# Turning attention results by VectorE block transposes instead of TensorE, with folded value biases and another order of events

## The chip, the cores and the metric

The kernel runs on one core of one Trainium2 chip. The metric is the device time of one execution in microseconds (us); the median of three runs is compared. A core has TensorE (PE, whose weight loads are listed as PEld), VectorE (DVE), ScalarE (ACT), GpSimd (POOL) and SyncE (SP), each with its own in-order queue of instructions, and semaphores between them.

## The reference

A decoder layer on `x` (4 batches x 512 tokens x 256) with a context of 4 x 1024 x 256: causal self attention, cross attention (16 heads of 16 each), and a mixture of 8 experts with the top 2 taken per token, each followed by a layer norm over the sum with its input.

```python
def _attn(q_in, k_in, v_in, wq, bq, wk, bk, wv, bv, wo, bo, causal):
    Q = (q_in @ wq + bq).reshape(Bq, Sq, H, HD)
    Kp = (k_in @ wk + bk).reshape(Bq, Sk, H, HD)
    V = (v_in @ wv + bv).reshape(Bq, Sk, H, HD)
    scores = jnp.einsum('bqhd,bkhd->bhqk', Q, Kp) / jnp.sqrt(jnp.float32(HD))
    ...
    a = jax.nn.softmax(scores, axis=-1)
    o = jnp.einsum('bhqk,bkhd->bqhd', a, V).reshape(Bq, Sq, Dm)
    return o @ wo + bo
x = _layernorm(x + _attn(x, x, x, ..., True), ln1_g, ln1_b)
x = _layernorm(x + _attn(x, ctx, ctx, ..., False), ln2_g, ln2_b)
x = _layernorm(x + _moe(x, ...), ln3_g, ln3_b)
```

All numbers are float32. Since the weights `a` of a row sum to 1, the value bias `bv` reaches the result as the constant row `bv @ wo`.

## The kernel before

**Work and tiles.** Attention is done in 32 units: 4 batches x self/cross x 4 groups of 4 heads (`UNIT_LIST`). A unit has key tiles of 128 keys: 4 in self attention, 8 in cross attention. For each unit

- `max` events: PE multiplies queries by keys into one of two PSUM slots (`v_slot`, L868/L872), DVE takes row maxima out of it (L1101), POOL and a transpose put them into the operand stack (`max_parts`, `max_rows`, `rows_in`).
- `score` events: PE computes one head's (or several heads') transposed scores of a key tile into one of three banks (`a_bank`, L896), ACT takes the exponential into `probs` (L1041).
- `weigh` events: PE adds the key tile's weighted values into `o_bank` (L913), four heads in four groups of 32 partitions (16 values, one sum of weights, 15 unused), 512 queries in the free dimension. There is one `o_bank`: the first `weigh` of the next unit waits until the last result was copied out.
- `o_out`, right behind a unit's last `weigh`: ACT copies `o_bank` to `o_sb` (L1051).
- `o_turn`, later: PE turns `o_sb` by four 128x128 transposes into a `v_slot` (L921), so that queries are in the partitions; DVE takes the reciprocal of the sums (L1120) and multiplies into `y` (L1123).

After a batch's fourth unit of a kind comes `att_turn`: PE turns `y` back by eight 128x128 transposes into two `a_bank`s (helper `transpose_y`, L816), ACT copies them to `o_t` and adds the value bias (L992). Then `out` multiplies `o_t` by `wo` (L935), DVE adds the residue (L1134), `stats` and `norm` do the layer norm, and `norm_turn` turns its result by the same helper for the next projection (`split`, L836, or `route`, L968). A `split` also goes through ACT (L1010, L1011), POOL (L705 to L709) and six DMAs into the operand stacks.

**Order.** All five queues walk through one list, `ORDER`. It is written out by hand as the string `STEPS`, one letter an event, each letter taking the next event of its track: `m` a maximum, `e` a score, `w` a weigh, `o` an `o_turn`, `r` `rows_in`, `a`, `k`, `v` projections, `s` and `c` the chains behind self and cross attention (which begin with `att_turn`). Other events are put behind named ones, `o_out` behind a unit's last `weigh` among them; `late_loads` issues the DMAs of `wo`, the result biases and others on SP behind the first three `rows_in`. The counters that tell which slot an event uses are worked out from this list in `Numbers`.

At the end, attention of the last batch runs into the experts: `weights` (steps of the routing weights, between DVE and ACT, L523 to L548) stands behind the last score, the last two `o_turn` behind the last `weigh`, then `att_turn`, then `first_row` (DVE copies a row tile, L1410, PE turns it, L1375), then `out`.

## Time and profile before

| | us |
|---|---|
| three runs | 999.18, 1001.68, 1002.14 (median 1001.68) |
| span of the profiled execution | 1004.4 |
| PE busy | 964.6 (96%), 6070 matmuls |
| DVE busy | 560.9 (56%), 957 instructions |
| ACT busy | 584.4 (58%), 1208 instructions |
| POOL busy | 340.8 (34%), 466 instructions |

The span runs from the first to the last instruction of one execution; no other time of that execution is shown, so its span is what sums are made against. "Busy" is the union of an engine's instructions. A matmul of float32 data shows as two instructions, a transpose as one. Matmuls overlap, since the next starts while the last one drains, so the mean duration of one is longer than the distance between two starts; the distance is what a matmul costs in a queue that is full. Attention ends with the start of the last `out` at 695.76 us; the rest is layer norm, routing and experts.

### The profile page before, as it was taken

The page shows a single profiled execution, that of the slowest core. Times are in us where ns is not written, and L with a number is a line of the kernel's source. Part 1 is how long each engine was busy: PE and PEld are TensorE (multiplying, and loading weights), DVE is VectorE, ACT ScalarE, POOL GpSimd, SP SyncE. Part 2 cuts the span into 40 slices and gives each one's busy share as a digit, 9 for nine tenths or more (in the row PEclk, how much of TensorE's full clock was granted, in tenths as well). Part 3 has the DMA queues.
Part 4 walks back from the last instruction along what each step waited for, and adds up shares of the span by engine and source line. Part 5 has one row for each costly group of instructions (what it writes and reads, how often), then busy time and mean ns, then how long its engine had stood idle before and what let it go on. Part 6 is the DMA issues. An engine that isn't in the chain of part 4 may idle for free.

```text
span 1004.4 us, 18852 instructions
## 1 busy us (share of the span) xinstructions
PE 964.6 (96%) x6070; PEld 577.6 (58%) x6071; DVE 560.9 (56%) x957; ACT 584.4 (58%) x1208; POOL 340.8 (34%) x466
## 2 busy tenths in 40 slices
PE   7899889999999999999999999999999999999995
PEld 4455534533445554434544354324888999999974
DVE  4637577787667677777777777852431222111216
ACT  3365456677766567776667866786333444444442
POOL 4465954233504542316254036021341111111115
PEclk9999999999999999999999999999999999999998
DMA  7633443002303201302515022011031443324116
GB/s 218 154 86 92 115 123 95 22 3 81 99 2 86 74 22 44 95 2 80 184 51 166 6 64 75 2 49 48 27 80 49 147 136 125 104 76 159 48 53 214
DMA packets 72013, 84.33 MB, mean 84 GB/s; under 512 B 10758, under 2 KB 65542, under 8 KB 71814
## 3 DMA queue, kind: packets, MB, share of 16 engines
q1 hardware_dynamic: 63820, 64.19, 22.3%
q0 software_dynamic: 5504, 17.34, 5.1%
q10 hardware_dynamic: 2624, 1.97, 0.7%
q8 instruction: 37, 0.61, 0.3%
q14 instruction: 28, 0.23, 0.1%
HBM read 38.89 MB, written 12.63 MB: 51 GB/s over the span
## 4 chain that ended last, share of the span: by engine, by line
PE 87%; DMA 4%; POOL 3%; DVE 2%; ACT 1%; issue 1%; SPq 1%; DVEq 0%; ACTq 0%; POOLq 0%; another core or an unknown queue 0%
PE o_bank L913 15%; PE a_bank L896 15%; PE v_slot L1393 12%; PE v_slot L868 11%; PE a_bank L1385 10%; PE a_bank L836 6%; PE v_slot L872 3%; PE o_bank L1385 3%; PE a_bank L851 3%; PE v_slot L935 3%; PE a_bank L816 1%; PE v_slot L873 1%; DMA stack_or_weights<-parts 1%; PE v_slot L921 1%; DVE max_q L1101 1%
## 5 line engine op out<-in xcount | busy, mean ns | idle before, releaser
L1101 DVE TENSOR_REDUCE max_q<-v_slot 128x1 f32<-128x1024 f32 (+3 forms) x352 | 399.1, 1172 | 100.4 <-PE v_slot L868 64.0
L1041 ACT ACTIVATE probs<-a_bank 128x512 f32<-128x512 f32 (+1 forms) x688 | 361.8, 589 | 114.0 <-PE a_bank L896 109.2
L1399 ACT ACTIVATE hidden<-a_bank,b 128x128 f32<-128x128 f32 x216 | 79.0, 367 | 147.8 <-PE a_bank L1385 127.1
L896 PE MATMUL a_bank<-q_stack_cross,k_stack_cross 99*128 99x512 bf16 x512 | 164.2, 381 | 0.5 <-ACT probs L1041 0.2
L868 PE MATMUL v_slot<-k_stack_cross,q_stack_cross 96*128 96x512 bf16 x512 | 148.6, 379 | 2.0 <-DMA q_stack_cross<-parts 2.0
L1393 PE MATMUL v_slot<-stack_or_weights,hidden 128*128 128x256 f32 x576 | 130.4, 379 | 1.1 <-DVEq L1225 1.1
L913 PE MATMUL o_bank<-probs,v_cross 128*32 128x512 f32 x1024 | 130.3, 602 | 0.0
L1393 PEld LDWEIGHTS v_slot<-stack_or_weights,hidden 128*128 128x128 f32 x576 | 106.6, 190 | 14.3 <-DVEq L1225 1.3
L1385 PE MATMUL a_bank<-x_col,stack_or_weights 128*128 128x128 f32 x864 | 109.2, 276 | 4.5 <-issue 2.4
L1385 PEld LDWEIGHTS a_bank<-x_col,stack_or_weights 128*128 128x128 f32 x864 | 104.8, 192 | 7.5 <-issue 5.6
L896 PEld LDWEIGHTS a_bank<-q_stack_cross,k_stack_cross 99*128 99x128 bf16 x512 | 44.5, 97 | 112.0 <-ACT probs L1041 66.5
L1546 POOL DMA_INDIRECT token_out<-y_row,to_i x28 | 26.7, 955 | 178.5 <-DVE y_row L1428 178.5
L868 PEld LDWEIGHTS v_slot<-k_stack_cross,q_stack_cross 96*128 96x128 bf16 x512 | 47.7, 98 | 62.6 <-issue 12.4
L705 POOL TENSOR_TENSOR rest<-rest,parts 128x512 f32<-128x512 f32 x39 | 45.1, 1156 | 95.0 <-ACT parts L1011 94.9
L1404 DVE COPY x_col<-v_slot 128x256 f32<-128x256 f32 x37 | 15.7, 425 | 106.5 <-PE v_slot L1375 99.8
L726 POOL CAST max_p<-max_q 128x16 bf16<-128x16 f32 x32 | 6.6, 208 | 185.8 <-DVE max_q L1101 185.8
L872 PE MATMUL v_slot<-stack_or_weights 96*128 96x128 bf16 (+3 forms) x256 | 59.9, 304 | 6.5 <-DMA stack_or_weights<-parts 2.8
L715 POOL TENSOR_SCALAR_AFFINE_SELECT probs<-probs 128x512 f32<-128x512 f32 x64 | 39.9, 637 | 58.0 <-ACT probs L1041 55.9
L896 PE MATMUL a_bank<-stack_or_weights 99*128 99x512 bf16 (+3 forms) x256 | 54.3, 302 | 2.9 <-DMA stack_or_weights<-max_t 2.5
L913 PEld LDWEIGHTS o_bank<-probs,v_cross 128*32 128x32 f32 x1024 | 23.1, 108 | 56.1 <-issue 28.7
L873 PE MATMUL v_slot<-mask_q,ident_b 128*128 128x128 bf16 x256 | 49.4, 222 | 0.0
L709 POOL TENSOR_TENSOR parts<-rest,parts 128x512 bf16<-128x512 f32 x39 | 45.4, 1164 | 3.1
(212 smaller groups left out, 1106.0 us busy)
## 6 DMA issues: line engine op xcount, KB each, us to landing
k_stack_cross<-parts SPq DMA_DIRECT2D x96, 128.0 KB, 2.4
stack_or_weights<-in_e_w SPq DMA_DIRECT2D x12, 1024.0 KB, 6.5
stack_or_weights<-parts SPq DMA_DIRECT2D x91, 128.0 KB, 2.4
q_stack_cross<-parts SPq DMA_DIRECT2D x48, 128.0 KB, 2.6
inputs<-in_ctxT POOLq DMA_DIRECT2D x4, 1024.0 KB, 6.6
stack_or_weights<-in_e_w SPq DMA_DIRECT2D x8, 512.0 KB, 4.2
x_slots<-slots_in SPq DMA_DIRECT2D x30, 129.0 KB
y_got<-token_out SPq DMA_DIRECT2D x11, 256.0 KB, 8.0
```

What stands on the lines that cost most here:

```text
L709: nc.gpsimd.tensor_tensor(parts[i][:, 2, :], rest[i][:, :], parts[i][:, 1, :], ALU.subtract).then_inc(split_done, 1)
L836: last = nc.tensor.matmul(bank[:, :], w[wname][:, kk, ch * P:(ch + 1) * P], src[:, kk, t0:t0 + S], start=(kk == 0), stop=(kk == DC - 1))
L868: last = nc.tensor.matmul(slot[:, half * S:(half + 1) * S], lhs, k_stack[1][0:KR, G * u + j, half * S:(half + 1) * S], start=True, stop=True)
L872: nc.tensor.matmul(slot[:, at:at + keys], lhs, k_stack[0][0:KR, G * u + j, 0:keys], start=True, stop=False)
L873: last = nc.tensor.matmul(slot[:, at + keys - P:at + keys], ident_b[:, :], mask_q[:, :], start=False, stop=True)
L896: last = nc.tensor.matmul(bank[:, i * cols:(i + 1) * cols], lhs, q_stack[kind][0:KM, G * u + j, q0:S], start=True, stop=True)
L913: last = nc.tensor.matmul(o_bank[32 * j:32 * (j + 1), q0:S], v_ext[kind][:, kt, at:at + 2 * HD], probs[NO.tile[n, kt] % PB][:, j, q0:S], s ...
L1041: nc.scalar.activation(probs[tile % PB][:, js[0]:js[-1] + 1, q0:S], a_bank[at % AS][:, 0:len(js) * (S - q0)].rearrange("p (j t) -> p j t", ...
L1101: nc.vector.tensor_reduce(most, rows, X, ALU.max, negate=True).then_inc(v_free, 1)
L1385: last = nc.tensor.matmul(h_bank[f % HB][:, 0:P], w1[i][:, c, f * P:(f + 1) * P], x_col[:, c, :], start=(c == 0), stop=(c == DC - 1))
L1393: last = nc.tensor.matmul(y_bank[:, 0:D], hidden[:, f, :], w2[i][:, f, :], start=(f == 0), stop=(f == FC - 1))
L1399: nc.scalar.activation(hidden[:, f, :], h_bank[f % HB][:, 0:P], ACT.Gelu, bias=b1[:, bass.ds(e * FC + f, 1)]).then_inc(flow.gelu_done, 1)
```

## The change

1. `o_out` goes from ACT to DVE: one block transpose of the whole `o_bank` (128 partitions x 512, each 32x32 block turned in place) into `o_tr`, an SBUF tile.
2. `o_turn` has no PE part and no `v_slot` any more. DVE takes the reciprocal of 16 sums and multiplies 256 numbers as before, but from `o_tr`, and writes in blocks of 32 queries to `o_n`, a view of `y`.
3. `att_turn` has no PE and no ACT part: DVE turns `o_n` back by two block transposes of 128x512 into `o_t`. `out` waits for these (`turned`).
4. The value biases are no longer added. A new event `value_biases` behind the fourth `rows_in` has ACT spread the two biases over 128 columns (4 instructions), PE multiply them by the two `wo` (4 matmuls of 256 columns), and DVE add the result to the rows of result biases `out_b`. `add_bias` of batch 0 on POOL waits for it.
5. The rows of `wo` and the value biases are permuted on the host so that two groups of heads share a block (`heads_in_blocks`).
6. `STEPS` is another string of the same events.

```diff
-            if k in ("max", "max_rows", "o_turn", "out", "route", "place"):
+            if k in ("max", "max_rows", "out", "route", "place", "value_biases"):
                 self.v[ev] = v
                 v += 1
...
@@ attention_gpsimd, add_bias
                     if b == 0:
                         pool.wait_ge(const_in, 16 * N_LOADS)
+                        pool.wait_ge(v_free, NO.v["value_biases",] + 1)
@@ attention_tensor
+                elif k == "value_biases":
+                    slot = v_next(ev)
+                    pe.wait_ge(rows_made, 2 * DC)
+                    pe.wait_ge(const_in, 16 * N_LOADS)
+                    for i, wname in enumerate(("sa_wo", "ca_wo")):
+                        for kk in range(DC):
+                            last = nc.tensor.matmul(slot[:, i * D:(i + 1) * D], bias_rows[:, i, kk, :], w[wname][:, kk, :], start=(kk == 0), stop=(kk == DC - 1))
+                    last.then_inc(v_full, 1)
...
-                elif k == "o_turn":
-                    n = ev[1]
-                    slot = v_next(ev)
-                    pe.wait_ge(o_out, n + 1)
-                    for q in range(QT):
-                        last = nc.tensor.transpose(slot[:, q * P:(q + 1) * P], o_sb[n % 2][:, q * P:(q + 1) * P], ident[:, :])
-                    last.then_inc(v_full, 1)
-                elif k == "att_turn":
-                    b, kind = ev[1:]
-                    pe.wait_ge(v_free, NO.v["o_turn", UNIT_NO[b, kind, UNITS - 1]] + 1)
-                    transpose_y(kind, NO.a[ev])
                 elif k == "out":
                     b, kind = ev[1:]
-                    pe.wait_ge(a_free, NO.a["att_turn", b, kind] + DC)
+                    pe.wait_ge(turned, DC * NO.turned[b, kind])
@@ attention_scalar
-                elif k == "o_out":
...
-                    sc.wait_ge(pv_done, NO.last_pv(b, kind, u) + 1)
-                    nc.scalar.activation(o_sb[n % 2][:, :], o_bank[:, :], ACT.Identity).then_inc(o_out, 1)
-                elif k == "att_turn":
-                    other_biases()
-                    to_o_t(NO.a[ev], "ca_bv" if ev[2] else "sa_bv")
+                elif k == "value_biases":
+                    other_biases()
+                    for i, n in enumerate(("sa_bv", "ca_bv")):
+                        for ch in range(DC):
+                            nc.scalar.activation(bias_rows[:, i, ch, :], ident[:, :], ACT.Identity, scale=0.0, bias=bias[n][:, ch:ch + 1]).then_inc(rows_made, 1)
@@ attention_vector
+                elif k == "o_out":
+                    n = ev[1]
+                    b, kind, u = UNIT_LIST[n]
+
+                    if n >= 2:
+                        dve.wait_ge(o_done, NO.o[n - 2] + 1)
+                    dve.wait_ge(pv_done, NO.last_pv(b, kind, u) + 1)
+                    nc.vector.transpose(o_tr[n % 2][:, :], o_bank[:, :]).then_inc(o_out, 1)
                 elif k == "o_turn":
...
+                    if kind and b == 0 and u == 0:
+                        dve.wait_ge(v_full, NO.v["value_biases",] + 1)
+                    dve.wait_ge(o_out, n + 1)
+                    heads = o_tr[n % 2][:, :].rearrange("p (n e) -> p n e", e=BLOCK)
+                    nc.vector.reciprocal(recip[n % 2][:, :], heads[:, :, HD]).then_inc(recip_done, 1)
+                    recips += 1
+                    dve.wait_ge(recip_done, recips)
+                    half = u % 2
+                    nc.vector.tensor_tensor(o_n[kind][:, u // 2, :].rearrange("p (n e) -> p n e", e=BLOCK)[:, :, half * HD:(half + 1) * HD],
+                                            heads[:, :, 0:HD], recip[n % 2][:, :].unsqueeze(2).to_broadcast([P, S // BLOCK, HD]),
+                                            ALU.mult).then_inc(o_done, 1)
+                elif k == "att_turn":
+                    b, kind = ev[1:]
+
+                    reader = NO.read_before[b, kind]
+                    if reader and reader[0] == "split":
+                        dve.wait_ge(a_full, NO.a[reader] + 1)
+                    elif reader:
+                        dve.wait_ge(v_full, NO.v[reader] + 1)
+                    dve.wait_ge(o_done, NO.o[UNIT_NO[b, kind, UNITS - 1]] + 1)
+                    for ch in range(DC):
+                        nc.vector.transpose(o_t[:, ch, :], o_n[kind][:, ch, :]).then_inc(turned, 1)
+                elif k == "value_biases":
+                    dve.wait_ge(v_full, NO.v[ev] + 1)
+                    slot = v_slot[NO.v[ev] % VS][:, 0:2 * D].rearrange("p (k d) -> p k d", k=2)
+                    nc.vector.tensor_tensor(out_b[:, :, :], slot, out_b[:, :, :], ALU.add).then_inc(v_free, 1)
@@ kernel
+def heads_in_blocks(v):
+
+    return v.reshape(DC, 2, G, HD, -1).swapaxes(1, 2).reshape(v.shape)
```

The first line of `STEPS`, before and after (13 lines in all; each letter stands as often as before, in another order):

```diff
-    "aavvaammmmmmammmrkmmmmaeeeammermeemewmeemeemweewweeemmmreemeeeemewwwwmmeaemoeeraeveeweeoeekwwweeemmeeemeememeemwowwwmmmra"
+    "aavvaammmmmmaammmrkmeememeemeeeewmmmeemwmreemweawemeeeeweeemrwwwaememaoemmeemeemeewemwomrmemeeemmeeemeweeweeewommrmwwwosa"
```

## Rows read from the trace of the kernel before

**Rows 1.** The page: busy time and share of PE; the chain by engine.

```profile
PE 964.6 (96%) x6070; PEld 577.6 (58%) x6071; DVE 560.9 (56%) x957; ACT 584.4 (58%) x1208; POOL 340.8 (34%) x466
...
PE 87%; DMA 4%; POOL 3%; DVE 2%; ACT 1%; issue 1%; SPq 1%; DVEq 0%; ACTq 0%; POOLq 0%; another core or an unknown queue 0%
```

**Rows 2.** Busy time by stretch: attention, the rest (engine busy, instructions, granted clock).

```profile
0.00:695.76 695.76, 674.24 (x4148) 310.93 (x4150) 479.12 (x663) 457.32 (x861) 278.99 (x403) 1.00 0.27 77
695.76:1004.40 308.64, 290.35 (x1922) 266.70 (x1922) 81.75 (x294) 127.05 (x348) 61.85 (x63) 0.99 0.31 100
```

**Rows 3.** Groups by shape (busy us, mean ns | idle before): what is removed.

```profile
L921 PE MATMUL v_slot<-ident,o_sb 128*128 128x128 f32 x128 | 19.7, 276 | 0.5 <-ACT o_sb L1051 0.5
L1051 ACT ACTIVATE o_sb<-o_bank 128x512 f32<-128x512 f32 x32 | 19.1, 598 | 20.1 <-PE o_bank L913 19.6 <-issue 0.3
L935 PE MATMUL v_slot<-self_weights,o_t 128*128 128x256 f32 x64 | 14.6, 380 | 0.0
L816 PE MATMUL a_bank<-ident,y_cross 128*128 128x128 f32 x64 | 8.4, 273 | 0.9 <-DVE y_cross L1123 0.9
L992 ACT ACTIVATE o_t<-a_bank,b_sa_bv 128x512 f32<-128x512 f32 x8 | 5.1, 684 | 0.9 <-PE a_bank L816 0.8
```

**Rows 4.** Timeline of PE around one `o_turn` (start, us, what).

```profile
305.84 0.60 PE L921 MATMUL v_slot<-ident,o_sb 128*128 128x128 f32 x4
306.28 0.33 PE L896 MATMUL a_bank<-stack_or_weights 99*128 99x384 bf16 x1
```

**Rows 5.** Groups by shape: DVE instructions nearest to the added ones.

```profile
L1101 DVE TENSOR_REDUCE max_q<-v_slot 128x1 f32<-128x1024 f32 x256 | 302.4, 1220 | 65.9 <-PE v_slot L868 64.0 <-issue 0.9
L1404 DVE COPY x_col<-v_slot 128x256 f32<-128x256 f32 x37 | 15.7, 425 | 106.5 <-PE v_slot L1375 99.8 <-remote 4.6 <-issue 2.1
L1101 DVE TENSOR_REDUCE max_q<-v_slot 128x4 f32<-128x512 f32 x16 | 11.1, 694 | 19.9 <-PE v_slot L873 19.8
L1120 DVE RECIPROCAL recip<-v_slot 128x16 f32<-128x16 f32 x32 | 8.2, 258 | 27.6 <-PE v_slot L921 21.4 <-PE a_bank L896 5.2
L1123 DVE TENSOR_TENSOR y_cross<-v_slot,recip 128x256 f32<-128x256 f32 x16 | 6.8, 424 | 0.6
```

**Rows 6.** Who waited for whom over the span (us in total, times, longest).

```profile
PEld a_bank L896 <- ACT probs L1041: 76.1, 126, 0.8
DVE max_q L1101 <- PE v_slot L868: 64.0, 107, 3.1
PEld v_slot L868 <- DVE max_q L1101: 9.2, 16, 0.8
```

**Rows 7.** Waits of others for the copy out of `o_bank`, L1051.

```profile
  PEld o_bank L913: 0.5, 1
```

**Rows 8.** Busy time, the 20 us stretch with a busy DVE (third number of busy).

```profile
640.00:660.00 20.00, 20.00 (x115) 5.98 (x113) 16.93 (x15) 15.87 (x30) 0.00 (x0) 1.00 0.01 2
```

**Rows 9.** Timeline of all engines at the end of attention.

```profile
689.50 1.64 PE L913 MATMUL o_bank<-probs,v_cross 128*32 128x512 f32 x12
690.34 0.26 DVE L534 TENSOR_REDUCE top_val<-logits 128x12 f32<-128x96 f32 x1 [14.34 <-ACT top_val L529]
691.07 0.66 PE L921 MATMUL v_slot<-ident,o_sb 128*128 128x128 f32 x4
...
692.07 0.18 DVE L548 TENSOR_TENSOR top_val<-top_val 128x12 f32<-128x12 f32 x1
...
692.98 0.26 DVE L1120 RECIPROCAL recip<-v_slot 128x16 f32<-128x16 f32 x1
693.27 0.42 DVE L1123 TENSOR_TENSOR y_cross<-v_slot,recip 128x256 f32<-128x256 f32 x1
693.61 0.28 DVE L1410 COPY x_row<-inputs 128x256 f32<-128x256 f32 x1
...
694.68 0.38 PE L1375 MATMUL v_slot<-ident,x_row 128*128 128x128 f32 x2
...
695.76 3.72 PE L935 MATMUL v_slot<-w_ca_wo,o_t 128*128 128x256 f32 x16 [0.70 <-ACT o_t L992]
```

**Rows 10.** Timeline of SP's queue: last of the late loads, fourth `rows_in`.

```profile
53.09 0.47 SPq L601 DMA_DIRECT2D router_b<-in_router_b  x1
...
66.09 0.76 SPq L612 DMA_DIRECT2D stack_or_weights<-max_t  x1
```

More of the change, by code:

```diff
@@ L38 @@
 SPLITS = 10
+BLOCK = 32
 AHEAD_ROWS = 4
@@ L192, in in_order @@
     order = spread
-    for step, behind in ((("result_biases",), ("norm_turn", B - 1, 0)), (("weights",), ("score", len(UNIT_LIST) - 1, ET - 1, score_groups(1, ET - 1)[-1], True)), (("pads",), ("choose", B - 2)), (("first_row",), ("att_turn", B - 1, 1)), (("experts", 0), ("norm", B - 1, 1)), (("experts", 1), ("route", B - 1)),
+    for step, behind in ((("value_biases",), ("rows_in", len(LATE))), (("result_biases",), ("norm_turn", B - 1, 0)), (("weights",), ("score", len(UNIT_LIST) - 1, ET - 1, score_groups(1, ET - 1)[-1], True)), (("pads",), ("choose", B - 2)), (("first_row",), ("att_turn", B - 1, 1)), (("experts", 0), ("norm", B - 1, 1)), (("experts", 1), ("route", B - 1)),
                          (("rank",), ("experts", 1)), (("experts", 2), ("rank",))):
@@ L218, in __init__ @@
                 a += 1
-            elif k in ("att_turn", "norm_turn"):
+            elif k == "norm_turn":
                 self.a[ev] = a
                 a += DC
+            elif k == "o_turn":
+                self.o[ev[1]] = len(self.o)
+            elif k == "att_turn":
+                self.turned[ev[1:]] = len(self.turned) + 1
+                self.read_before[ev[1:]] = reader
+            if k in ("out", "route") or k == "split" and ev[2] >= 8:
+                reader = ev
             if k == "split":
```

58 lines of the change are left out of this document (27 added, 31 removed).

## The prediction

> **What bounds the kernel now.** I read the page's busy times and its chain first, then busy time by stretch, then groups by shape, then who waited for whom, last the timelines of single places. The reader is to see PE at 96% of the span and on 87% of the chain that ended last, every other engine below 60% [rows 1]. By stretch it is plainer: while attention runs (0 to 695.76 us) PE is busy 674.2 us, DVE 479.1 (69%), ACT 457.3 (66%), and the clock granted to PE is full, 1.00 [rows 2]. So what leaves PE's queue shortens the time, as long as no other queue steps into its place. Behind 695.76 the change touches nothing but the start of the last `out`.
>
> PE's busy time hides short waits: its weight loads waited 76.1 us in total for the exponentials on ACT, in 126 places of at most 0.8 us, mostly while the last matmul drained [rows 6]. DVE on the contrary waited for PE's maxima 64.0 us in 107 places, and PE for DVE's slots 9.2 us in 16 (cross units; self units not counted here) [rows 6]. DVE has room, on the average.
>
> **Removed from PE.** The `o_turn`s are 32 x 4 = 128 transposes. Their busy time is 19.7 us [rows 3], but in a full queue four of them take 306.28 - 305.84 = 0.44 us from start to next start [rows 4]: 32 x 0.44 = 14.1 us. The `att_turn`s are 8 x 8 = 64 of the same shape (half of two groups like the L816 row of [rows 3]; the other half is `norm_turn` and stays): 64 x 0.11 = 7.0 us. Together 21.1 us; by busy time it would be 19.7 + 8.4 = 28.1, which is the upper end.
>
> **Added to PE.** `value_biases` is 4 matmuls of 256 columns, shown as 8; 64 such take 14.6 us [rows 3], so 8 x 0.23 = 1.8 us. Its waits: the late loads, whose last is issued at 53.09, 13 us before the fourth `rows_in` at 66.09, behind which the event stands [rows 10]; in the new list some 12 us of PE work lie between the third and the fourth. I take no wait; were the landing 5 us late, 5 us. Queued behind that wait on PE is everything, so nothing hides it. POOL's first `add_bias` then waits for it too, with splits and masks behind; in the new list `out` of batch 0, which needs the sum, is 14 us of PE work later. The four ACT instructions write 128 columns each; below 4 x 0.6 (the 512-column one of [rows 3]), and `y_cross`, where they write, is otherwise first written in cross attention. Nothing. DVE's sum is one instruction more, 0.7. PE's net is 21.1 - 1.8 = 19.3 us.
>
> **Moved from ACT to DVE.** ACT loses 32 copies of 0.598 and 16 of 0.684 [rows 3], 19.1 + 10.9 = 30 us of its 457. DVE gains 32 block transposes out of PSUM and 16 out of SBUF, each 128x512; the `o_turn` pair (0.258 + 0.424 [rows 5]) stays. The trace has no such transpose. From below: a DVE copy of 256 columns takes 0.425, the reduction of 512 columns 0.694 [rows 5]; a fast copy of 256 columns 0.28 [rows 9], so not below 0.56. From above: as dear as a reduction of 1024 columns, 1.22 [rows 5]. I take 0.69, since one pass over 512 columns is what it is. 48 x 0.69 + 0.7 = 34 us: DVE 479 + 34 = 513 in some 678 us, 76%. In its busiest stretch (16.93 of 20 us [rows 8]) it comes to about 90%.
>
> The Trainium skill speaks to this price and to the change itself: "VectorE: DVE Perf Modes", The three transpose paths, gives 311 ns for a VectorE transpose of 128x128 bf16, in 32x32 blocks only, against 390 on TensorE, and its rules for kernel authors send a 128x128 transpose to TensorE. Four such would be an estimated 1.24 us, near my upper end; no row here has the operation. The 390 is a latency: this trace has 0.276 as the mean and 0.11 as what a transpose costs in a full PE queue [rows 3, 4]. By the page's figures the sum is that of the second rival below.
>
> **The wait that is added.** PE's first `weigh` of the next unit now waits for DVE, where the transpose stands behind maxima, instead of ACT. Before, PE waited 0.5 us once for that copy [rows 7]. I counted PE work in the new list between a unit's last `weigh` and the next unit's first: 31 gaps, from 0.64 to 24 us, median 1.9 (before 3.0); 16 are below 2.0, 18 below 3.2. With DVE idle 0.8 is needed; two gaps of 0.64 then cost 0.3 together. With one maximum under way, 1.22 + 0.69 + 0.1 = 2.0 is needed, and the gaps fall short by 7.2 us in all. But in the new list a last `weigh` (1.0 us) nearly always has another `weigh` or two scores ahead of it and no maximum within the last 1.4 us, so the DVE is mostly free when it ends. I take a quarter: 2 us. While DVE stands waiting for `pv_done`, maxima wait behind it, but PE has one slot more free than before, since `o_turn` uses none. DVE's `att_turn` waits for the last reader of `o_t`, an event earlier on PE; nothing.
>
> **The end of attention.** Here nothing covers the chain, and the reader has to walk it [rows 9]. Before: last `weigh` done at 691.07, `out` starts at 695.76. After, DVE does the steps of `weights` first (they stand before the last `weigh`; the last ends at 692.07 + 0.18 = 692.25), and only then the transpose (692.94), two pairs of reciprocal and product (from 692.98 to 693.27 to the end at about 693.71, so 0.73 each: 694.40), two transposes (695.78), the row copy 0.28 (696.06), and PE's two transposes of that row with the semaphores, 0.4: `out` at 696.45. That is 0.7 later than before, though PE lost 0.44 x 2 + 0.87 = 1.75 there that stands in my 21.1. Correction: -2.45. With transposes at 1.22 it is another 1.6.
>
> **Sum.** 19.3 - 2.45 - 2 = 14.9 us off the profiled span: 1004.4 - 14.9 = 989.5. The runs' median lies 2.7 below that span (1001.68), so I forecast 986.8, say 986. Bounds of it: net PE 26 instead of 19 by busy time, 980; a wait for loads or dearer transposes, 992.
>
> The order itself I cost at nothing: PE works through the same multiplications, and DVE's and ACT's shares by stretches of 25 us look alike but for DVE's gain. That is the weakest term.
>
> **Rivals.**
>
> 1. *ACT's relief comes through too, 977.* ACT has 30 us less, and PE's loads waited 76 us for it [rows 6]. If an eighth of those waits, 9.5 us, was real and goes, the time is 986.5 - 9.5. For: at 640 to 660 ACT and DVE are both near 80% or more [rows 8]. Against: the waits are short and lie under draining matmuls, and DVE grows as ACT shrinks.
> 2. *The block transpose costs 1.22.* 48 x 0.53 = 25 us more on DVE, 79% busy, near 100% in its full stretches. If a third comes through, 8.5, and 1.6 at the end: 986.5 + 10 = 997. For: nothing in the trace shows a transpose. Against: one pass over the data.
> 3. *DVE holds `o_bank`: slower, 1012.* If at each last `weigh` two maxima are queued on DVE, 2 x 1.22 + 0.69 + 0.1 = 3.2 us are needed, 18 gaps are short of it, by 27.5 us in all. 1004.4 - 16.9 + 27.5 - 2.7 = 1012. It decides from 16.9 / 31 = 0.55 us of stall per unit. For: the median gap shrank from 3.0 to 1.9. Against: the maxima stand earlier in the list, and PE's wait for ACT in the same place was 0.5 in all [rows 7].
> 4. *The new order loses what the rest gains, about 1001*: a row of maxima or a load that lands late in the first 70 us, where PE was not full.
>
> **How the numbers follow.** Forecast (981 to 992) 0.60; rival 1 0.14; rival 2 0.12; rival 3 0.10, of which half is above 1005; rival 4 0.04. The likeliest gives 986. A measurement of this kernel can tell about 0.3%, 3 us, from no change: below 998.7 is faster. Forecast and rival 1, and most of 2, lie there: 0.85; same 0.06 (rival 4, the mild end of 2 and 3); slower 0.09. The range that leaves out no more than 2 in 10 goes from 975 (rival 1) to 999 (rival 2 and the mild end of 3).
>
> **What would show it.** Right: PE's busy time in attention down by about 19 us or more, no L921, 64 transposes at L816 instead of 128; DVE transposes near 0.7 us; the last `out` starting about 15 us sooner, and the stretch behind it the same 308.6 us [rows 2]; waits of PE for the transpose out of `o_bank` of 1 to 4 us in sum. Wrong: transposes above 1 us; many waits of the first `weigh` for DVE; PE idle where `value_biases` stands; a change of over 2 us behind the last `out`.

## The result: 0.9% slower, where 1.6% faster was forecast

The changed kernel took 1009.92 us (median of 5 runs, 1008.03 to 1015.29) beside 1001.69 (5 runs of the kernel before on the same chip, 999.18 to 1003.67): ratio 1.0088, interval 1.0063 to 1.0113. The forecast was 986 (975 to 999). The profiled execution has a span of 1007.9 us against 1004.4.

The page of the kernel after: busy time by engine, and the chain that ended last.

```profile
PE 959.8 (95%) x5886; PEld 556.0 (55%) x5887; DVE 594.2 (59%) x1006; ACT 561.2 (56%) x1164; POOL 341.9 (34%) x466
...
PE 85%; DVE 4%; DMA 4%; POOL 2%; issue 2%; ACT 1%; SPq 1%; DVEq 0%; POOLq 0%; ACTq 0%
```

Its busy time by stretch, cut where the last `out` (L948 now) starts. The columns are as in [rows 2].

```profile
0.00:699.18 699.18, 667.34 (x3965) 286.83 (x3966) 511.51 (x710) 434.96 (x818) 280.01 (x403) 0.99 0.27 76
699.18:1007.90 308.72, 292.50 (x1923) 269.15 (x1922) 82.72 (x296) 126.26 (x346) 61.94 (x63) 0.98 0.32 101
```

Set beside [rows 1, 2]: attention ends 3.4 us later, and the stretch behind the last `out` is as long as before (308.7 against 308.6), though the two are not made alike: after the change 3.0 us of it are lost to half clock, before it none. PE has 183 instructions less there, and yet its busy time fell by 6.9 us, not by 19, since a matmul's busy time stretches with the clock and with the ones before it. DVE rose by 32.4 us, as forecast (34). ACT fell by 22.4, less than my 30.

The groups of the kernel after that answer to [rows 3, 5]: `o_turn`'s PE transposes are gone, and these came.

```profile
L1122 DVE STREAM_TRANSPOSE o_tr<-o_bank 128x512 f32<-128x512 f32 x32 | 22.8, 712 | 13.9 <-PE o_bank L937 13.5
L1138 DVE TENSOR_TENSOR y_cross<-o_tr,recip 128x256 f32<-128x256 f32 x16 | 9.5, 595 | 0.5
L1138 DVE TENSOR_TENSOR y_self<-o_tr,recip 128x256 f32<-128x256 f32 x16 | 8.1, 509 | 0.6
L1151 DVE STREAM_TRANSPOSE o_t<-y_cross 128x512 f32<-128x512 f32 x8 | 5.2, 688 | 0.3 <-DVE route_space L511 0.2
```

The price of a block transpose was foreseen: 0.712 us out of PSUM and 0.688 out of SBUF, against 0.69, so the second rival's 1.22 didn't come about. The product, costed at the 0.424 of [rows 5], has a mean of 0.55.

Who waited for whom over the span of the kernel after (total us, times, longest), answering to [rows 6, 7].

```profile
PEld a_bank L920 <- ACT probs L1053: 99.0, 173, 0.8
DVE max_q L1107 <- PE v_slot L884: 52.5, 94, 3.3
PEld v_slot L884 <- DVE max_q L1107: 12.4, 25, 0.8
```

PE's loads now wait 99.0 us for the exponentials instead of 76.1, in 173 places instead of 126. Most of that is the new list: the kernel before with only the list replaced (e2 below) already has 95.7 us up to the last `out`, and the new turns with the old list (e1) have 81.4.

**One account for all the kernels.** Busy time can't tell work from waiting here, so I worked another out of each trace: the distance from each matmul's start to the next one's, up to the last `out`. The usual distance of the same pair of shapes in the same kernel is *work*. The length of the stretches in which the record of the granted clock says half (1.2 in place of 2.4 GHz) counts by half, as *half clock*. What is over, where it is above 20 ns, is *waits*. Some 5 to 7 us (PE's first start and smaller rests) are left in every kernel. The last column comes from all runs of a kernel and not from its profile: the median of a run's span times its mean granted clock, which takes half-clock time away from the whole run in the same way. For the kernel before it is 992.8 to 993.4 in the batches of 10 to 23 runs that stood beside the experiments. A star marks kernels whose experts get other rows; their last column can't be compared with the others.

```
                                     last out  work   half clock  waits   span x clock
before                                 695.8   656.1     1.7       31.5       993.0
after                                  699.2   639.5     8.9       44.1       992.8
e1  new turns, old list                702.1   638.5     8.9       49.7       995.7
e2  old turns, new list                728.3   656.5    13.7       51.6      1016.2
e3  e1 + idle PE transposes            718.4   657.3    10.2       44.4      1010.6
e4  e1, ACT copies o_bank              706.2   639.0    11.1       51.7       997.2
e5  e1, biases later                   701.1   636.7     8.4       49.2       996.2
e6  e1, half the transposes            693.4   637.1     5.1       45.1      993.6*
e7  before + 60.5 us idle DVE          727.1   656.1     8.8       55.6      1016.8
e8  before + folded biases             700.6   657.8     3.4       32.9       997.6
e9  e1 without biases                  694.4   635.0     3.4       49.3      985.3*
e10 e1, biases in PE's waits           699.4   634.6    10.1       48.1       993.1
e11 e10 + end of attention reordered   694.0   636.8     1.7       48.7       992.5
e12 e11 with the new list              700.5   638.4    10.4       45.4       993.6
e13 before + 33 us idle DVE            702.3   656.0     5.1       34.8       997.2
e14 before + end reordered             693.6   656.0     1.7       29.3       993.7
e15 e11 + PE kept at work at the end   691.6   639.2     1.7       43.8       993.1
e16 before, a quarter of the turns     687.4   640.6     2.0       38.7      989.8*
e17 e16 + 33 us idle DVE               696.4   638.7     5.1       46.3      995.6*
```

After against before: 16.6 us of work went, 7.2 of half clock and 12.6 of waits came, 3.4 in all with the rests. The turns alone went down by 20.8 (26.9 to 6.1), near my 21.1; the biases gave 1.7 back (e8). The other 2.5 are not accounted for (e2 has 0.4 more work than before, after has 1.0 more than e1). The split hangs on what is called usual: with the distance that 15% of a pair's lie below, after against before is 14.7 less work and 13.3 more waits, so work and waits are good to about 2 us against each other.

Two things in this table have to be kept in mind. First, over all runs the changed kernel isn't slower once half-clock time is taken away (992.8 against 993.0): its mean granted clock has a median of 0.985, that of the kernel before 0.990 to 0.992. By this count the loss is all half clock, and freed work, new waits and biases come out even. It is good to a microsecond or so: the clock is given to three decimals, and the clocks of the five runs of the kernel before beside the result aren't on record. Second, each line but for the last column is one execution, and the one of the kernel before isn't typical. Its span times its clock is 999.7, where none of its runs with a clock on record is above 995.5. Part of that lies behind the last `out`, which takes 308.6 us with no half clock at all, where the other kernels with the same rows have 304 to 306 without theirs. Another 2.2 us lie between the 29th and the 54th microsecond: e14, with the same instructions as before up to the last unit, is ahead by that much there and stays so. Differences of 2 to 3 us between two lines of the table can be chance.

### The profile page after: what moved, and what is told of

Its sections match the earlier page's. It is cut to its first block, busy times and chain, and to the rows that moved or that the text cites. A ratio compares the mean times of both kernels' runs of the same rounds, so it can differ in the third digit from the quotient of the medians.

```text
span 1007.9 us, 18427 instructions
## 1 busy us (share of the span) xinstructions
PE 959.8 (95%) x5886; PEld 556.0 (55%) x5887; DVE 594.2 (59%) x1006; ACT 561.2 (56%) x1164; POOL 341.9 (34%) x466
## 3 DMA queue, kind: packets, MB, share of 16 engines
q1 hardware_dynamic: 63820, 64.19, 22.4%
## 4 chain that ended last, share of the span: by engine, by line
PE 85%; DVE 4%; DMA 4%; POOL 2%; issue 2%; ACT 1%; SPq 1%; DVEq 0%; POOLq 0%; ACTq 0%
PE o_bank L937 15%; PE a_bank L920 14%; PE v_slot L1423 12%; PE v_slot L884 11%; PE a_bank L1415 9%; PE a_bank L852 6%; PE a_bank L867 4%; PE o_bank L1415 3%; PE v_slot L888 3%; PE v_slot L948 3%; DVE max_q L1107 2%; PE v_slot L889 1%; DMA q_stack_cross<-parts 1%; DMA inputs<-in_ctxT 1%; PE v_slot L1405 1%
## 5 line engine op out<-in xcount | busy, mean ns | idle before, releaser
L937 PE MATMUL o_bank<-probs,v_cross 128*32 128x512 f32 x1024 | 132.9, 606 | 0.5 <-DVE o_tr L1122 0.5
L1576 POOL DMA_INDIRECT token_out<-y_row,to_i x28 | 26.9, 959 | 181.2 <-DVE y_row L1458 181.2
L937 PE MATMUL o_bank<-probs,v_self 128*32 128x128 f32 (+3 forms) x512 | 46.5, 462 | 3.4 <-POOL probs L730 2.8
```

Source lines behind the costliest of these rows:

```text
L937: last = nc.tensor.matmul(o_bank[32 * j:32 * (j + 1), q0:S], v_ext[kind][:, kt, at:at + 2 * HD], probs[NO.tile[n, kt] % PB][:, j, q0:S], s ...
```

## Experiments

**First round: which part.** e1 has the new turns and folded biases with the `STEPS` of before; e2 is the reverse, the kernel before with only `STEPS` replaced.

> The changed kernel (block transposes on VectorE, folded value biases) with the list of events of the kernel before. Theory O (the new list costs the time: in the trace of the changed kernel TensorE lost 19 us of transposes but its stalls before the last out grew from 31 to 44 us and its half-clock time from 3.4 to 17 us, most of it at places with another neighbourhood in the list): 983 to 990 us, stalls near those of before, one or two half-clock stretches. Theory D (VectorE's new work is what stalls TensorE, whatever the list): 1003 us or more.

> The kernel before (TensorE transposes, ScalarE copies, value biases added as before) with the new list of events. Theory O: slower than before by what the list costs, 1012 to 1025 us, with more half-clock stretches than one. Theory D: within 5 us of before, 997 to 1006 us.

e1: 1012.14 against 1004.71, ratio 1.0082 (1.0052 to 1.0112). e2: 1031.63, ratio 1.0267 (1.0244 to 1.0291). e1's time is in theory D's range, e2's above the ranges of both theories. With the new turns the new list is worth 0 to 3 us (699.2 against 702.1), so the loss is in the turns and biases. With the old turns it costs 32 us at the last `out` and 27 in the medians (the execution that was profiled was the slowest of its six). A list that serves the new turns does harm with the old ones.

**Second round: PE's work, `o_bank`, the biases' place, the transposes' size.**

```diff
# e3: PE does as many idle transposes into v_slot as it lost
+ fill(slot)      # QT owed by each o_turn, DC*QT by each att_turn
# e4: ACT copies o_bank, DVE turns the copy in SBUF
- nc.vector.transpose(o_tr[n % 2][:, :], o_bank[:, :]).then_inc(o_out, 1)
+ nc.scalar.activation(o_tr[n % 2][:, :], o_bank[:, :], ACT.Identity).then_inc(o_out, 1)
+ nc.vector.transpose(o_tr[n % 2][:, :], o_tr[n % 2][:, :]).then_inc(blocks_turned, 1)
# e5: ("value_biases",) and ("add_bias", 0) behind ("o_turn", 3)
# e6: the block transposes take 256 of 512 columns (from unit 2 on)
```

> New turns in the old list, and TensorE gets as many transposes back as it lost (128 and 64, of the identity, written into the next slot before the real matmuls overwrite them, with no wait of their own). If TensorE's work sets the pace in this list: 19 us above the new turns in the old list (ratio to before 1.026 to 1.029). If what was taken off TensorE was only turned into waits: the filler goes into those waits and keeps the clock up, 0 to 6 us above (ratio 1.005 to 1.014).

> New turns in the old list, but the result bank is copied out by ScalarE as before, and VectorE turns the copy in place at the o_turn event: the same VectorE work, no longer between the last weigh and the next unit's first one. If VectorE's hold on the result bank costs: 4 us or more below the new turns in the old list (ratio to before 1.004 or less). If it is VectorE's load, wherever it stands: within 3 us of it (ratio 1.005 to 1.011).

> New turns in the old list, value_biases and the first add_bias moved from behind the fourth rows_in to behind the fourth o_turn, some 20 us of TensorE work later. In the trace of the new turns in the old list 6 us of lag against before arise at value_biases (wait, its matmuls at half clock). If that lag lasts: 4 to 6 us below it (ratio 1.002 to 1.004). If later waits swallow it: within 2 us (ratio 1.006 to 1.010).

> New turns in the old list, each block transpose over 256 of the 512 columns (but for the first two units), so half of the queries' results are stale: VectorE has about 13 us less work, all else the same. If VectorE's added load is what TensorE waits for: 6 us or more below the new turns in the old list (ratio to before 1.002 or less). If VectorE's load is hidden: within 2 us (ratio 1.006 to 1.010).

e3: 1025.0 against 1002.83, ratio 1.0215 (1.0177 to 1.0252), a span 16.5 us above e1's. PE's work does count, even with DVE loaded: 16.3 us at the last `out` for 18.8 us of work put back, though the ratio lies between the two ranges that I had. e4: 1017.43, ratio 1.0143 (1.0099 to 1.0187), the last `out` 4.1 us later than in e1: DVE's hold on `o_bank` (my third rival) isn't the cause, and the copy on ACT costs more than it frees. The ratio is above both ranges; 2.2 of the 4.1 us are half clock. e5: 1012.01, ratio 1.0093 (1.0064 to 1.0123), no gain, as its second theory had it. e6: 1008.93, ratio 1.0077 (1.0049 to 1.0106): 10.6 us less of DVE's time (579.8 busy against 590.4) brought the last `out` 8.7 us nearer, 3.8 of it half clock and 4.6 waits. The ratio is in the range of "hidden" all the same: the stale queries give the experts other rows, and the stretch behind the last `out` takes 312.0 us instead of e1's 307.8. Only the last `out` may be compared, and that is one execution, the fastest of six.

**Third round: the suspects alone.** e7 is the kernel before with VectorE transposes that nobody reads. e8 is the kernel before with only the biases folded. e9 is e1 without the biases.

```diff
# e7 (in DVE's list, behind pv_done of each unit and at att_turn)
+ for i in range(3 if k == "o_out" else 10):
+     nc.vector.transpose(spare[:, :], w["ca_wk"][:, i % 2, 0:160]).then_inc(spare_done, 1)
```

> The kernel before, its list, its turning on TensorE and its biases untouched; VectorE is given, at the places of the change's block transposes, about the same time of work that nobody reads (three transposes of 160 columns in SBUF behind each last product with the values, ten at each att_turn, each waiting for the one before: some 0.3 us each, 32 x 3 + 8 x 10 = 176 of them, near 40 us in all). THEORY LOAD (VectorE has no room in time: each 0.7 to 2.8 us in which it doesn't take score maxima is a wait of TensorE somewhere, because TensorE's buffers of the mask scores are two deep): 1010 to 1018 us, the stalls of the matmuls up to the last out up by 8 to 15 from 31.5. RIVAL START AND CLOCK (the cost sits in the value biases at the start and in the half-clock stretches, VectorE's extra work is hidden in its idle third): within 3 us of the kernel before. RIVAL TAIL: only the four late transposes count: 2 to 3 us.

> The kernel before, its list and its turning on TensorE, with one part of the change: the value biases folded into the result biases (eight ACT rows, eight more matmuls right behind the last late rows, one VectorE add; the evictions at att_turn lose their bias operand, nothing else). THEORY START (TensorE stands about 2 us for the ACT rows and runs its four-byte matmuls at the half clock, and the start is not made up later): 1006 to 1009 us, lag of 4 to 6 us against before at the 68th microsecond and still there at the last out. RIVAL LOAD (slack behind the start takes it up, the loss is made by VectorE's transposes): within 2 us of before.

> The new turns with the list of before, as in the first experiment, with the value biases left out altogether (no ACT rows, no matmuls for them; the result lacks these biases). THEORY START: 1003 to 1007, 5 to 9 us below the first experiment. THEORY LOAD: 1008 to 1012, within 3 us of the first experiment, as TensorE waits for VectorE in the middle all the same. Were both costs gone with it, as in my forecast, it would be at 985.

e7: 1035.46 against 1003.61, ratio 1.0319 (1.0295 to 1.0343). In its trace the transposes come to 60.5 us, not to the near 40 that I had meant; the last `out` came 31.3 later, and the time is far above theory load's range. The tile's line, and three of PE's waits up to the last `out` (before, the first was 76.1 in 126 places and the second 9.2 in 16 [rows 6]):

```profile
L1121 DVE STREAM_TRANSPOSE spare<-w_ca_wk x176: 331/345/348, 52.3 to 726.0; 128x160 f32<-128x160 f32 x176
```

```profile
PEld a_bank L898 <- ACT probs L1043: 76.2, 126, 0.8
...
PEld v_slot L870 <- DVE max_q L1104: 25.8, 35, 3.4
...
PE v_slot L870 <- DVE max_q L1104: 7.9, 9, 2.9
```

DVE's load shows where its maxima empty PE's slots, and ACT's wait stays at 76. But the cost isn't spread over the 60 us. Each matmul set beside the same one in the kernel before shows where the lag grows: by 22 us at the eight blocks of ten, which hold DVE for 3.75 us each, and by 7 at the 32 blocks of three, 1.1 us each. One block of ten, and the matmuls that then stand for a slot:

```profile
325.34 3.75 DVE L1121 STREAM_TRANSPOSE spare<-w_ca_wk 128x160 f32<-128x160 f32 x10
...
329.75 0.60 PE L870 MATMUL v_slot<-k_stack_cross,q_stack_cross 96*128 96x512 bf16 x2 [1.69 <-DVE y_self L1137]
```

So e7 prices mostly a DVE held for 3.75 us at a stretch, which the change doesn't do: its longest pair of block transposes takes 1.30.

e8: 1010.23, ratio 1.0070 (1.0045 to 1.0095). Four ACT rows (I had written eight), four PE matmuls and a DVE sum cost 4.8 us at the last `out`, inside theory start's lag of 4 to 6 (its time was a microsecond short), and the lag is all there by the 155th microsecond and stays. Here they are in e1: first PE, then ACT.

```profile
61.81 0.60 PE L920 MATMUL a_bank<-stack_or_weights 99*128 99x512 bf16 x2
64.59 2.05 PE L903 MATMUL v_slot<-self_weights,y_cross 128*128 128x256 f32 x4 [2.17 <-issue]
66.43 1.91 PE L903 MATMUL v_slot<-w_ca_wo,y_cross 128*128 128x256 f32 x4
...
61.19 0.68 ACT L1023 ACTIVATE parts<-a_bank,b_sa_bq 128x512 bf16<-128x512 f32 x1
61.76 1.57 ACT L1053 ACTIVATE probs<-a_bank 128x512 f32<-128x512 f32 x3
63.20 0.70 ACT L1062 ACTIVATE y_cross<-ident,b_sa_bv 128x128 f32<-128x128 f32 x2
63.79 0.70 ACT L1062 ACTIVATE y_cross<-ident,b_ca_bv 128x128 f32<-128x128 f32 x2
```

The rows stand behind a split's copies and three exponentials and end at 64.49. PE starts at 64.59, after 2.17 us of idling; the profile names no releaser, the times fit the rows. The record of the clock then has 6.8 us at 1.2 GHz from the 63rd microsecond: the eight records take 3.75 us from 64.59 on, where I had 1.8.

e9: 998.35, ratio 0.9949 (0.9935 to 0.9964), but that ratio misleads: without the biases the router chooses other rows, and the stretch behind the last `out` is 301.9 us instead of 308.6. Only the last `out` may be compared: 694.4 against e1's 702.1, nearly all of it (7.1) there by the 155th microsecond. The biases cost 7.7 us there, 5.5 of it half clock, and the new turns without them gain 1.4 on the kernel before, not 20. As a time, 998.35 is below the ranges of both theories.

**Fourth round: mending it.**

```diff
# e10: ("value_biases", 0), self half, ahead of ("score", 1, 0, ...)
#      ("value_biases", 1), cross half, ahead of ("out", 0, 0)
#      ACT's rows behind ("mask", 0, 1)
# e11: e10, and DVE's list at the end of attention
- o_out 30, ..., weights, o_out 31, o_turn 30, o_turn 31, att_turn, copy_row
+ o_out 30, o_turn 30, copy_row, o_out 31, o_turn 31, att_turn, weights
# e12: e11 with the changed kernel's STEPS (the same end)
```

> The new turns with the list of before, and the value biases complete, but in two halves that stand where TensorE waits anyway: the self half (two matmuls) ahead of unit 1's first score, where PE stood 2.4 to 3.6 us for a transfer of max_t at the 45th microsecond, the cross half ahead of the first out, where it stood 1.56 us for o_t; the ACT rows earlier, beside unit 0's exps. THEORY PLACE (what the fold cost was its place: the wait, the half-clock stretch behind it, and what it pushed): as fast as with no biases at all, 998 to 1001 us, PE not waiting at either half for more than it did before. RIVAL WORK (rows, matmuls and adds cost as work wherever they stand): 1004 to 1012, as in the first experiment. RIVAL CLOCK CHANCE (half-clock stretches come and go with any shift of the timing, as when the fold was only put later): anywhere from 998 to 1012, with stretches in other places.

> The kernel of the tenth experiment with the end of attention put in another order: unit 30's reciprocal and product ahead of unit 31's last products with the values, the copy of x_row behind them, and the seven small steps of the expert weights on VectorE behind the last four block transposes, not ahead of them. THEORY TAIL (TensorE's 4.6 us wait ahead of the last out is a chain on VectorE, 1.8 us of weights' steps, 0.66 of unit 30, 0.25 of the row, then 0.71, 0.66 and 1.3 of unit 31's own): the wait falls to about 2.5 us, 2 to 3 us below the tenth: 995 to 998. RIVAL GIVEN BACK (the weights, later now, or the first gelu and its table load, hold the experts): within 1 us of the tenth.

> The kernel of the eleventh with the changed kernel's list of events in place of that of before: the whole change, with the two repairs. THEORY (the list is worth nothing here, the repairs the same as on the old list): the changed kernel's 1009.9 less 10 to 13 = 997 to 1000 us. RIVAL (the new list has other waits at the halves' places, so that they aren't hidden there): 1001 to 1008.

e10: 1007.59 against 1003.88, ratio 1.0037 (1.0016 to 1.0058). The waits are those of e9 (48.1, 49.3), so the fold no longer makes any; but the profiled execution had 6.8 us at 1.2 GHz at the 24th microsecond, where no other kernel of that list has it, and 6.8 more at the 696th. e11: 1002.64, ratio 0.9992 (0.9969 to 1.0015). e12: 1012.59, ratio 1.0096 (1.0073 to 1.0118), with the 24th's stretch again. Theory place holds for the waits, but its time (998 to 1001) was missed: 1007.59 lies in the ranges of both rivals. Without half clock e10 is at 993.1 over all runs, e1 at 995.7. e11 and e12 missed their times too (995 to 998, and 997 to 1000 or the rival's 1001 to 1008): the repairs on the new list gained nothing that the runs show. From the end of the last `weigh` to `out` it is 4.9 us in e9 and 3.1 in e11, so theory tail has 1.8 of its 2 to 3; beside it the two profiled executions differ by 8.4 us of half clock. Over all runs the medians are 5.0 apart, and only 0.6 without half clock.

How much of it changes from run to run shows in e11's twelve: the mean granted clock goes from 0.996 (998.03 us) to 0.985 (1007.29). One place of the expert stage has the same wait in two kernels. First the kernel before, then e11.

```profile
768.14 1.60 PE L1385 MATMUL a_bank<-x_col,stack_or_weights 128*128 128x128 f32 x12 [2.01 <-DVEq L1666]
```

```profile
766.20 2.14 PE L1432 MATMUL a_bank<-x_col,stack_or_weights 128*128 128x128 f32 x12 [2.04 <-DVEq L1713]
```

The same 2.0 us of idling: at 2.4 GHz behind it in the one, at 1.2 in the other. The length of the wait alone doesn't decide.

**Fifth round: size, end, clock.** e13 is e7 with two transposes behind each unit and four at each `att_turn` (96, 33 us, the change's own size). e14 is the kernel before with e11's order of the end. e15:

```diff
  elif k == "first_row":
      transpose_row(pe, early, 0)
+     pe.wait_ge(a_free, LAST_SCORE + 1)
+     for i in range(11):
+         nc.tensor.matmul(a_bank[LAST_SCORE % AS][:, 0:P], ident[:, :], ident[:, :], start=True, stop=True)
```

> As the seventh experiment (kernel before, TensorE's turns and biases kept), with idle transposes on VectorE of the change's own size: two of 160 columns behind each unit, four at each att_turn, 96 at 0.344 us = 33 us. THEORY LINEAR (half a microsecond of TensorE's waits for each of VectorE's, as 60.5 us cost 31): 16 to 18 us slower than before, 1019 to 1022. RIVAL THRESHOLD (VectorE has room for the first 30, the seventh kernel went past it): under 6 us slower. With theory linear the whole sum of the change is closed: -16.5 of TensorE's work, +16 of waits for VectorE, +5 to 7 of the biases and the end.

> The kernel before with the reordering of the end of attention alone (unit 30's product ahead of unit 31's last weigh, the copy of x_row behind it, the small steps of the expert weights behind the last turns). In before's trace these steps ran from 690.34 to 692.16, while TensorE still turned unit 30 (to 691.7), and unit 31's turn came from TensorE at 692.8: THEORY HIDDEN THERE: 0 to 1 us faster (unit 31's turn no longer waits behind unit 30's, which TensorE also does earlier). RIVAL AS IN THE ELEVENTH (the same edit was worth 5 us in the median there): 3 to 5 us faster, so a version that beats both.

> The eleventh kernel with eleven idle 128x128 four-byte matmuls into a free score bank in TensorE's 2.9 us wait ahead of the last out, where the kernel before had its eight turns. THEORY CLOCK (the out behind that wait ran 5.41 us at 1.2 GHz for part of it, against 3.72 in the kernel before with the same sixteen matmuls; work in the gap keeps the 2.4 GHz): out takes 3.7 us again, no stretch at the 695th, 1.7 us faster than the eleventh (1000 to 1001 in its rounds), TensorE's wait for o_t under 1 us. RIVAL (the fall comes from elsewhere or from later): out at 5.4 us again, no change, or slower by the matmuls if they outlast the gap.

e13: 1012.06 against 1003.96, ratio 1.0064 (1.0041 to 1.0087); 6.5 us at the last `out`, 3.3 of them waits and 3.4 half clock. Theory linear falls; rival threshold (under 6) is nearer, but 6.5 is above it. 33 us cost 6.5 and e7's 60.5 cost 31.3, for the length of e7's blocks as said there: here blocks of four hold DVE for 1.5 us, and all eight of them cost 2. Without half clock all runs are 3.9 us above the kernel before. e14: 1003.78, ratio 0.9994 (0.9977 to 1.0012): no difference that these runs tell, and its lead of 2.1 at the last `out` is that from the start. e15: 1002.39, ratio 0.9984 (0.9967 to 1.0000). In e11 the last `out` opened at half clock behind an idle PE:

```profile
690.89 0.44 PE L1422 MATMUL v_slot<-ident,x_row 128*128 128x128 f32 x2
694.02 5.41 PE L959 MATMUL v_slot<-w_ca_wo,o_t 128*128 128x256 f32 x16 [2.70 <-DVE o_t L1164]
```

The sixteen records of `out` take 5.41 us there. In e15, with work in the gap, they take the 3.72 of the kernel before [rows 9], and the record of the clock has no stretch there:

```profile
688.44 0.44 PE L1426 MATMUL v_slot<-ident,x_row 128*128 128x128 f32 x2
688.72 2.62 PE L975 MATMUL a_bank<-ident 128*128 128x128 f32 x22
691.58 3.72 PE L960 MATMUL v_slot<-w_ca_wo,o_t 128*128 128x256 f32 x16 [0.24 <-DVE o_t L1168]
```

All the traces agree. In the nine other executions with the new turns and a PE without work there (after, e1, e4 to e6, e9 to e12) a stretch at 1.2 GHz lies over the last `out`; in the four of the old turns with neither transposes taken from PE nor load put on DVE (before, e2, e8, e14) none does. In e7, e13, e16 and e17 one does, and in e3 one ends 0.7 us ahead of the last `out`. So the transposes that the change took from PE's end had also kept its clock. e15 starts its last `out` 4.2 us before the kernel before does (2.0 before e14 does). Over whole runs it can't be told from the kernel before or from e11.

**Sixth round: four corners.** In e16 and e17 each `o_turn` and `att_turn` does one transpose of four.

```diff
- for q in range(QT):      # o_turn, and transpose_y at att_turn
+ for q in range(1):       # DVE and ACT read these 128 columns four times
```

> The kernel before with one TensorE transpose where there were four, in o_turn and att_turn (the columns of the first 128 queries are read for all four tiles, so the attention results of the other queries are wrong and the experts get other rows: only the start of the last out is to be compared, 695.8 in the kernel before). 144 transposes of some 0.11 us less, 15 to 16 us of TensorE's work, nothing else changed on VectorE or ACT but the reads. THEORY TENSORE BOUNDS (freed time is time): last out at 679 to 682. THEORY INTERACTION (half of it comes back as waits for VectorE and ACT, which were just ahead of TensorE): 684 to 690.

> The same with the thirteenth's 33 us of idle transposes on VectorE: the fourth corner, and the change without its biases. THEORY ADDITIVE (the two don't touch): the sixteenth plus 3 to 7 us. THEORY INTERACTION (VectorE's load costs more the less TensorE has to do): the sixteenth plus 9 to 14, near the 694.4 of the ninth experiment, with 12 or more of waits above the thirteenth's 34.8.

e16: last `out` at 687.4, e17: at 696.4 (whole runs 1005.7 and 1010.06, ratios 1.0013, 0.9990 to 1.0036, and 1.0050, 1.0028 to 1.0072, but with other rows for the experts). The corners, by the last `out` and the waits:

```
                     turns on PE       a quarter of them
no load of DVE      695.8   31.5        687.4   38.7
33 us of load       702.3   34.8        696.4   46.3
```

15.5 us of PE's work taken away brings 8.4: 7.2 come back as waits, with nothing else changed. It isn't the chance of one place: up to the 80th microsecond the two executions are within 0.2 us of each other, and the gain grows from 0.6 us at the 130th to 8.0 at the 683rd. PE's loads up to the last `out` waited for ACT 82.1 us there instead of 76.1:

```profile
PEld a_bank L896 <- ACT probs L1045: 82.1, 143, 0.8
```

The load of DVE costs 6.5 us alone and 8.9 beside the lighter PE, and its waits are 3.3 and 7.6. Theory interaction holds for e16, inside its range. For e17 nothing is settled. At the last `out` 8.9 is just under interaction's range (9 to 14) and above the additive one (3 to 7), but 2.4 us between four single executions is about the size of the chance seen above, and e16's profiled one was the fastest of its ten (1000.7, median 1005.7). The medians of whole runs say the reverse, 8.1 us alone and 4.4 beside the lighter PE; without half clock they are 3.9 and 5.8. The fourth corner, the change's turns by parts, is at 696.4; the real ones without biases (e9) were at 694.4.

## Why the prediction was wrong

The sum from the corners, each at the last `out`, profiled executions: the lighter PE -8.4, DVE's load +8.9, the biases +7.7 (e1 less e9), together +8.2 where e1 has +6.3. The 1.9 between them are what the real turns, with ACT relieved, do otherwise than their stand-ins, and chance. The new list took 2.9 off: +3.4. The medians of the runs are 8.2 apart and not 3.4, because the profiled execution of the kernel before was a long one: its span is 1004.4, and that of the median run 1000.0 (a run's time is 1.7 above its span).

- **"So what leaves PE's queue shortens the time, as long as no other queue steps into its place."** This is the step that failed first. I checked the place at `o_bank` alone. In e16, where nothing but PE's transposes went, 7.2 of 15.5 us came back as waits all over the list, mostly of less than a microsecond, and PE's loads waited 6.0 us longer for ACT. With the real turns PE's loads wait 10.4 us longer for the maxima on DVE (`v_slot <- max_q`, 9.2 to 19.6 in e1) and 5.3 longer for ACT. 96% busy made PE look like the only bound; its 126 waits for ACT of at most 0.8 us [rows 6] were the mark of a second engine just ahead of it.
- **The turns' own size** was right: 21.1 forecast, 20.8 by the account.
- **"DVE has room, on the average"** and 34 us at no price. The size was right (32.4 in attention), the price wasn't: 6.5 alone (e13), 8.9 with the lighter PE (e17), of which 3.4 and 3.1 are half clock. My own line, 90% in its busiest stretch, should have carried a price.
- **"I take no wait"** for `value_biases`, and ACT's rows "Nothing": 2.17 us of waiting in e1 that end with just those rows, though not for the late loads as I had feared, and PE's part at half clock. Forecast 1.8, measured 4.8 (e8) to 7.7 (e9). The mistake is of a kind: I asked where `y_cross` is written, and not what ACT has in its queue ahead of the rows.
- **The clock** stood in no term. It grew by 7.2 us up to the last `out`, more than the whole 3.4 there, it is 5.5 of e1's 7.7 for the biases, and over all runs it is the whole loss, by the last column of the table. At the end of attention its cause is shown, an idle PE (e15 and the traces named beside it). For the other stretches it is open. Why the 24th microsecond has one in e2, e10 and e12 alone stays open too, and so does the share of chance: one profile of each kernel has it as it fell.
- **The wait for `o_bank`, 2 us,** was about right: PE waited 1.1 us for `o_tr` at its matmuls. Rival 3, the only one on the slower side, had nearly the right time (1012) by a wrong mechanism; e4 speaks against it. Rival 1, ACT's relief, didn't show in PE's waits for ACT, which grew by 5.3 us in e1; but they grew by 6.0 in e16, where ACT isn't relieved, and e4, which gives ACT its copies back, is 4.1 us later than e1. What the relief is worth was not tested by itself.
- **The end of attention** was walked rightly. The chain after:

```profile
692.01 2.09 PE L937 MATMUL o_bank<-probs,v_cross 128*32 128x512 f32 x16
...
695.03 0.18 DVE L563 TENSOR_TENSOR top_val<-top_val 128x12 f32<-128x12 f32 x1
695.13 0.71 DVE L1122 STREAM_TRANSPOSE o_tr<-o_bank 128x512 f32<-128x512 f32 x1
...
697.16 1.30 DVE L1151 STREAM_TRANSPOSE o_t<-y_cross 128x512 f32<-128x512 f32 x2
698.39 0.25 DVE L1440 COPY x_row<-inputs 128x256 f32<-128x256 f32 x1
...
698.70 0.69 PE L1405 MATMUL v_slot<-ident,x_row 128*128 128x128 f32 x2 [4.59 <-DVE x_row L1440]
...
699.18 2.34 PE L948 MATMUL v_slot<-w_ca_wo,o_t 128*128 128x256 f32 x5
```

  From the last `weigh`'s end (694.1) to `out` are 5.1 us; I had 5.4 (691.07 to 696.45). The small steps of the expert weights stand before the transpose, as the reader of [rows 9] could see; moving them behind it, with unit 30's product and the row's copy ahead (e11), took 1.8 off. What I didn't see is that `out`, behind 4.6 us of an idle PE, would open at half clock.
- **"The order itself I cost at nothing"**: about right with the new turns, 2.9 in its favour; with the old ones 32 us against it.

## What to carry to other kernels

An engine that is 96% busy while two others wait for it and make it wait in turn, in a hundred places of half a microsecond, is not the only bound: take time off it and expect a part (here about half), and price each microsecond that goes onto a neighbour, above all where it holds that neighbour for long at a stretch (e7's blocks of 3.75 us). Whether the price rises as the first engine gets lighter these runs don't settle. Walk the queue of every engine that feeds an inserted step, since a preparation of 0.4 us may stand behind 2 us of others' work. Work taken from an engine's idle end may have been what kept its clock; look at the granted clock behind every wait that an edit makes longer. And before single profiles are subtracted, see whether the profiled execution is a typical one: here the base of all differences wasn't.

## What the runs showed of the hardware that was not expected

- The product of VectorE, 0.424 us in the kernel before in every case, reads SBUF now in place of PSUM and was up to six times as long beside a GpSimd instruction. From e1's timeline:

```profile
69.21 2.17 POOL L755 TENSOR_TENSOR x_all<-x_all,out_b 128x1024 f32<-128x1024 f32 x1 [3.53 <-issue]
69.26 2.40 DVE L1138 TENSOR_TENSOR y_self<-o_tr,recip 128x256 f32<-128x256 f32 x1
```

  The kernel after has 17.6 us of products where 13.6 stood before. All ten of its products over 0.43 us began while a GpSimd instruction was under way, and each ended 0.27 to 0.29 us behind the end of one. The kernel before, whose products read PSUM, has 17 beside GpSimd instructions and none over 0.426.
- Behind like waits of 2.0 us PE ran once at 2.4 and once at 1.2 GHz. The runs of one kernel spread by more than the 0.3% that I had gone by, and mostly with their granted clock: e11's go from 998.03 us (0.996) to 1008.38 (0.987).
- A VectorE transpose of 160 columns takes 0.344 us, one of 512 columns 0.688, both in SBUF: about 0.19 us fixed and 0.98 ns for each column (two points, so the split is worked out, not measured).
